# First attention of a twelve-stage decoder: the weighing moves between the second and the third turning, and ScalarE's second copy moves behind three exponentials

## The chip, the cores and the metric

The kernel runs on one core of a Trainium2 chip. The metric is the device time of one launch in microseconds (us); less is better. The times shown are the median, the lowest and the highest of three runs. Engines: TensorE (PE in the profile, and PEld for its weight loads), VectorE (DVE), ScalarE (ACT), GpSimd (POOL), and SyncE (SP), which issues the loads.

## The reference

A decoder of four layers, each with self-attention, cross-attention and a feed-forward part, over x of 4 batches, 512 positions and 128 features. Only the first self-attention is touched by the change. Per batch and with x normalised:

```
qkv = x @ W_attn + b_attn                    # 16 heads of 8 features
att = (q @ k.T) / sqrt(8) / temperature
att = att + slope[h] * (pos_k - pos_q), and -inf where pos_k > pos_q
w = softmax(att, axis=-1)
x = x + (w @ v) @ W_proj + b_proj
```

## The kernel before

The stages run one after the other; the first attention is the first of them, `l0_attention`. Its inner work is cut into 64 quads. Quad k belongs to batch b = k // 16, to query tile tt = (k % 16) // 4 of 128 queries, and to group g = k % 4. It holds four heads r = 0 to 3 (`R`), and works on the (tt + 1) * 128 keys that the causal mask leaves, so that a quad of tt = 3 is four times as wide as one of tt = 0. In this text quad number n of a batch is k % 16.

Each quad passes through these steps:

- `score` on TensorE (L415): four matmuls, one for each head, into banks 0 to 3. It waits until all four masks of the quad before are done.
- `mask` on VectorE (L240), one for each head: adds the position bias, takes the row minimum and writes `sc`.
- `exponent` on ScalarE (L353), one for each head: writes `pr`.
- `turn` on TensorE (L426), one for each head: (tt + 1) transposes of 128x128 into one of two banks. Heads 0 and 2 share bank 4 and heads 1 and 3 share bank 5, so a turning waits for the copy of the turning before it in its bank.
- `copy`, which frees the bank: heads 0 and 2 on ScalarE (L345), heads 1 and 3 on VectorE (L250). It writes `prT`, of which there are two sets (`RING` = 2).
- `weigh` on TensorE (L443 and L447): probabilities times v, and times ones for the sums. It waits for all four copies of its quad.
- After every fourth quad VectorE divides (reciprocal L267, product L271) once `weigh` of that quad's fourth group is done. It does so at the head of its iteration k, three quads later, ahead of `mask(k, 0)`; that is where k % 4 = 2, from k = 6 on.

The steps are ordered by one loop written out on each engine, each with its own program of iterations k, and semaphores between them. In iteration k TensorE scores quad k, turns quad k - 1 and weighs quad k - 2. VectorE masks quad k and copies quad k - 1. ScalarE copies quad k - 1 and takes the exponentials of quad k.

In iterations with n = 4 to 12 of the first three batches one piece of the next batch's projection is done as well (`project`, L394, and for the ninth, v, L397). For the first eight pieces ScalarE then takes the result out of its bank (`take`, L327 and L330, which waits for the projection) and rounds it (`round_high`, L337), and GpSimd finishes it. VectorE takes the ninth out. In iteration n = 3 of each later batch, and once after the last quad, TensorE also does the output projection of the batch before (L471), and VectorE adds it to X (L290).

Of the kernel before, what the change touches and what calls it, by code (L numbers as in the profile page):

```python
# [159 lines left out]
def l0_attention(nc, T, A):  # L160
    H, HD = 16, 8
    G, R = 4, 4
    QUADS = B * TPB * G
# [6 lines left out]
    with Stage(nc, T, "l0a") as st:  # L170
# [32 lines left out]
        def place(k):  # L203

            b, n = divmod(k, PER)
            return b, n // G, n % G

        def piece_at(k):

            b, n = divmod(k, PER)  # L210
            return [(b + 1, n - FIRST)] if b + 1 < B and 0 <= n - FIRST < PIECES else []

        def home(b, n):

            return T.bank[n % 8] if b == 0 else pbank

        with nc.Block() as block:
# [96 lines left out]
            @block.scalar  # L314
            def _(act):
                def take(b, n):

                    g, kind = divmod(n, 2)
                    act.wait_ge(projected, PIECES * b + n + 1)
                    done = 2 * G * b + n - 4  # L320
                    if done >= 0:
                        if kind:
                            act.wait_ge(split_k, done // 2 + 1)
                        else:
                            act.wait_ge(split_q, done // 2 + 1)
                    if kind:
                        nc.scalar.activation(raw[:, n % 4, :], home(b, n)[:, :], ACT.Identity, bias=cols[:, G + g:G + g + 1])\  # L327
                            .then_inc(taken, 1)
                    else:
                        nc.scalar.activation(raw[:, n % 4, :], home(b, n)[:, :], ACT.Identity, bias=qbias[:, g:g + 1],  # L330
                                             scale=qscales[:, g:g + 1]).then_inc(taken, 1)

                def round_high(b, n):

                    g, kind = divmod(n, 2)
                    act.wait_ge(taken, 2 * G * b + n + 1)
                    nc.scalar.activation(qk[:, b % 2, kind, g, :], raw[:, n % 4, :], ACT.Copy).then_inc(high, 1)  # L337

                def copy(j, r):

                    W = (place(j)[1] + 1) * P
                    act.wait_ge(turned, R * j + r + 1)
                    if j >= RING:
                        act.wait_ge(pv_done, j - RING + 1)
                    nc.scalar.activation(prT[:, j % RING, r, 0:W], tbank[0][:, 0:W], ACT.Copy).then_inc(copied_a, 1)  # L345

                def exponent(k, r):

                    W = (place(k)[1] + 1) * P
                    act.wait_ge(masked, R * k + r + 1)  # L350
                    if k >= RING:
                        act.wait_ge(turned, R * (k - RING) + r + 1)
                    nc.scalar.activation(pr[:, k % RING, r, 0:W], sc[:, k % RING, r, 0:W], ACT.Exp,  # L353
                                         bias=nmx[:, k % RING, r:r + 1], scale=-1.0).then_inc(expd, 1)
                act.wait_ge(loaded, 16 * len(loads))
                act.wait_ge(prepared, 1)
                for n in range(2 * G):
                    take(0, n)
                    if n:
                        round_high(0, n - 1)  # L360
                round_high(0, 2 * G - 1)
                for k in range(QUADS + 1):
                    if k >= 1:
                        copy(k - 1, 0)
                    if k < QUADS:
                        exponent(k, 0)
                    if k >= 1:
                        copy(k - 1, 2)
                    if k < QUADS:
                        for r in range(1, R):  # L370
                            exponent(k, r)
                    for b, n in piece_at(k):
                        if n < 2 * G:
                            take(b, n)
                            round_high(b, n)

            @block.tensor
            def _(pe):
# [22 lines left out]
                def score(k):  # L401

                    b, tt, g = place(k)
                    W = (tt + 1) * P
                    if tt == 0:
                        pe.wait_ge(split_q, G * b + g + 1)
                        pe.wait_ge(split_k, G * b + g + 1)
                    if k >= 1:
                        pe.wait_ge(masked, R * k)
                    else:  # L410
                        pe.wait_ge(taken, 2 * G)
                        pe.wait_ge(v_ready, 1)
                    for r in range(R):
                        m = slice(32 * r, 32 * r + 32)
                        out = nc.tensor.matmul(sbank[r][:, 0:W], qk[m, b % 2, 0, g, tt * P:(tt + 1) * P], qk[m, b % 2, 1, g, 0:W],  # L415
                                               start=True, stop=True)
                    out.then_inc(scored, 1)

                def turn(j, r):

                    pe.wait_ge(expd, R * j + r + 1)
                    before = 2 * j + r // 2
                    if before:
                        pe.wait_ge(copied_v if r % 2 else copied_a, before)
                    for t in range(place(j)[1] + 1):
                        out = nc.tensor.transpose(tbank[r % 2][:, t * P:(t + 1) * P], pr[:, j % RING, r, t * P:(t + 1) * P],  # L426
                                                  T.ident[:, :])
                    out.then_inc(turned, 1)

                def weigh(j):  # L430

                    b, tt, g = place(j)
                    pe.wait_ge(copied_a, 2 * j + 2)
                    pe.wait_ge(copied_v, 2 * j + 2)
                    if tt == 0 and g == 0:
                        pe.wait_ge(v_ready, b + 1)
                    if g == 0 and j // G >= 1:
                        pe.wait_ge(yT_ready, j // G)
                    for t in range(tt + 1):
                        first, end = g == 0 and t == 0, g == G - 1 and t == tt  # L440
                        for r in range(R):
                            m, c = slice(32 * r, 32 * r + 32), r * G * STRIDE + g * R * HD
                            nc.tensor.matmul(obank[m, 0:P], v[:, b % 2, t, c:c + R * HD],  # L443
                                             prT[:, j % RING, r, t * P:(t + 1) * P], start=first, stop=False)
                        for r in range(R):
                            m = slice(32 * r, 32 * r + 32)
                            out = nc.tensor.matmul(obank[m, P:2 * P], ones[:, g * R * HD:(g + 1) * R * HD],  # L447
                                                   prT[:, j % RING, r, t * P:(t + 1) * P], start=False, stop=end)
                    out.then_inc(pv_done, 1)
# [4 lines left out]
                for k in range(QUADS + 4):  # L454
                    if k < QUADS:
                        score(k)
                    for r in range(R if 1 <= k <= QUADS else 0):
                        turn(k - 1, r)
                    for b, n in piece_at(k):
                        project(b, n)  # L460
                    if 2 <= k < QUADS + 2:
                        weigh(k - 2)
                    if k >= PER and k % PER == 3:
                        b = k // PER - 1
                        pe.wait_ge(yT_ready, TPB * b + TPB)
                        if b + 1 < B:
                            pe.wait_ge(v_ready, b + 2)
                        else:
                            pe.wait_ge(added, b)
                        for t in range(TPB):  # L470
                            out = nc.tensor.matmul(pbank[:, t * D:(t + 1) * D], yT[:, b % 2, t * P:(t + 1) * P], wproj[:, :],  # L471
                                                   start=True, stop=True)
                        out.then_inc(out_ready, 1)
# [2128 lines left out]
```

## Time and profile before

| | us |
|---|---|
| median of 3 runs | 2660.39 (2655.98 to 2660.68) |
| the profiled execution's own time | 2660.01 |
| its span, first to last instruction | 2658.2 |
| first score of the stage to first score of its last quad | 32.5 to 288.6 |
| last weighing of the stage ends, reciprocal starts | 299.8 |

The span is made of stages with different limits; the first attention is a tenth of it. Its quads have no loads from memory in them, so that they are read from the timeline of the three engines. What sets a quad's length is the distance from one `score` to the next.

### The profile page before, as it was taken

The page shows a single profiled execution, that of the slowest core. Times are in us where ns is not written, and L with a number is a line of the kernel's source. Part 1 is how long each engine was busy: PE and PEld are TensorE (multiplying, and loading weights), DVE is VectorE, ACT ScalarE, POOL GpSimd, SP SyncE. Part 2 cuts the span into 40 slices and gives each one's busy share as a digit, 9 for nine tenths or more (in the row PEclk, how much of TensorE's full clock was granted, in tenths as well). Part 3 has the DMA queues.
Part 4 walks back from the last instruction along what each step waited for, and adds up shares of the span by engine and source line. Part 5 has one row for each costly group of instructions (what it writes and reads, how often), then busy time and mean ns, then how long its engine had stood idle before and what let it go on. Part 6 is the DMA issues. An engine that isn't in the chain of part 4 may idle for free. (4 is left out here: it accounts for less than half of the span.)

```text
span 2658.2 us, 43969 instructions
## 1 busy us (share of the span) xinstructions
PE 2227.7 (84%) x13502; PEld 1582.2 (60%) x13502; DVE 1791.3 (67%) x3827; ACT 1241.8 (47%) x2557; POOL 1196.4 (45%) x1377
## 2 busy tenths in 40 slices
PE   6888759663999975749999999989999867699698
PEld 3666547453788853636656556655666445499555
DVE  4667658556688856666776676767677555477598
ACT  6777535222566642225445344534444432244365
POOL 5331028001699920127666565756575100022298
PEclk8999869775999998769999999999999977699799
DMA  1000024000666600013344343334333400000184
GB/s 45 2 2 2 7 57 100 7 6 19 140 153 153 150 4 18 1 63 80 80 84 92 77 98 75 96 65 96 77 84 79 87 6 0 32 1 1 25 176 101
DMA packets 63008, 162.17 MB, mean 61 GB/s; under 512 B 7563, under 2 KB 18571, under 8 KB 55000
## 3 DMA queue, kind: packets, MB, share of 16 engines
q1 hardware_dynamic: 62792, 159.50, 26.8%
q8 instruction: 110, 1.80, 0.3%
q14 instruction: 106, 0.87, 0.1%
HBM read 156.46 MB, written 3.01 MB: 60 GB/s over the span
## 5 line engine op out<-in xcount | busy, mean ns | idle before, releaser
L1984 PE MATMUL bank<-l2h_og,l2h_wo 128*128 128x512 f32 x512 | 264.2, 600 | 12.0 <-DVE LNT L2228 11.3
L2086 ACT ACTIVATE l2h_pr<-twin,l2h_nmx 128x512 f32<-128x512 f32 x256 | 176.0, 688 | 173.6 <-PE bank L1973 122.3
L2078 ACT ACTIVATE l2h_prT<-bank 128x512 f32<-128x512 f32 x256 | 151.7, 592 | 213.1 <-PE bank L1973 213.1
L1075 POOL TENSOR_TENSOR l1m_hid_lo<-l1m_hid,l1m_hid_hi 128x512 fp32r<-128x512 f32 x136 | 217.2, 1617 | 62.1 <-ACT l1m_hid_hi L1054 61.4
L2231 DVE TENSOR_REDUCE l2h_nmx<-twin 128x2 f32<-128x1024 f32 x128 | 156.2, 1220 | 104.5 <-PE twin L1963 103.8
L2204 DVE TENSOR_TENSOR l2h_vg<-bank,l2h_gv 128x512 f32<-128x512 f32 x256 | 175.4, 685 | 54.6 <-POOL l2h_vs L2299 32.0
L2299 POOL TENSOR_TENSOR l2h_vs<-l2h_vg 128x256 f32<-128x256 f32 x256 | 190.8, 745 | 27.9 <-DVE l2h_vg L2204 27.7
L2294 POOL TENSOR_TENSOR l2h_plain<-l2h_plain,l2h_rotated 128x512 f32<-128x512 f32 x64 | 82.0, 1281 | 213.9 <-DVE l2h_rotated L2197 213.9
L2216 DVE TENSOR_TENSOR l2h_og<-bank,l2h_gt 128x512 f32<-128x512 f32 x256 | 173.2, 680 | 5.3 <-PE bank L1984 2.7
L1973 PE MATMUL bank<-ident,l2h_pr 128*128 128x128 f32 x1024 | 163.4, 282 | 2.5 <-issue 2.5
L1973 PEld LDWEIGHTS bank<-ident,l2h_pr 128*128 128x128 f32 x1024 | 119.0, 143 | 71.4 <-issue 54.8
L1948 PE MATMUL bank<-l2h_w_hi,l2h_x_hi 128*128 128x512 f32 x256 | 151.5, 592 | 4.8 <-DVE l2h_vg L2204 3.7
L1114 DVE TENSOR_TENSOR l1m_hid<-l1m_prod,l1m_c 128x512 f32<-128x512 f32 x128 | 132.5, 1035 | 5.6
L2302 POOL TENSOR_TENSOR l2h_vs<-l2h_vs 128x128 f32<-128x128 f32 x256 | 124.2, 485 | 20.1
L353 ACT ACTIVATE l0a_pr<-l0a_sc,l0a_nmx 128x128 f32<-128x128 f32 (+3 forms) x256 | 128.9, 553 | 8.0 <-DVE l0a_nmx L240 7.7
L426 PE MATMUL bank<-ident,l0a_pr 128*128 128x128 f32 x640 | 105.3, 288 | 29.7 <-ACT l0a_prT L345 23.6
L118 PE MATMUL bank<-ident,LNX 128*128 128x128 f32 x112 | 27.6, 425 | 119.3 <-ACT LNX L127 98.7
L1048 ACT ACTIVATE l1m_gate<-bank 128x512 f32<-128x512 f32 x136 | 81.3, 598 | 93.7 <-PE bank L1009 93.7
L1997 PE MATMUL bank<-l2h_prT,l2h_v 128*64 128x256 f32 x1024 | 124.6, 385 | 0.0
L1984 PEld LDWEIGHTS bank<-l2h_og,l2h_wo 128*128 128x128 f32 x512 | 95.4, 190 | 43.2 <-issue 18.1
L1075 POOL TENSOR_TENSOR l3m_hid_lo<-l3m_hid,l3m_hid_hi 128x512 fp32r<-128x512 f32 x68 | 107.8, 1615 | 27.8 <-ACT l3m_hid_hi L1054 27.6
L2307 POOL TENSOR_TENSOR l2h_v<-l2h_vs 128x64 f32<-128x64 f32 x256 | 83.0, 324 | 71.4 <-PE bank L1997 53.7
(636 smaller groups left out, 6199.1 us busy)
## 6 DMA issues: line engine op xcount, KB each, us to landing
l2h_gt<-l2m_gate_rows SPq DMA_DIRECT2D x128, 512.0 KB, 7.1
l1m_c<-l1m_weights SPq DMA_DIRECT2D x64, 512.0 KB, 6.3
l3m_c<-l3m_weights SPq DMA_DIRECT2D x32, 512.0 KB, 6.6
l0m_c<-l0m_weights SPq DMA_DIRECT2D x16, 512.0 KB, 6.8
l1m_w<-in_l1m_pairs SPq DMA_DIRECT2D x32, 192.0 KB, 6.2
l2h_fresh<-in_l2m_wqkv SPq DMA_DIRECT2D x8, 768.0 KB, 4.9
l2h_wo<-in_l2m_wo SPq DMA_DIRECT2D x8, 512.0 KB, 4.8
l0m_w<-in_l0m_pairs SPq DMA_DIRECT2D x8, 192.0 KB, 5.0
```

The costliest lines, as they stand in the source:

```text
L353: nc.scalar.activation(pr[:, k % RING, r, 0:W], sc[:, k % RING, r, 0:W], ACT.Exp, bias=nmx[:, k % RING, r:r + 1], scale=-1.0).then_inc(exp ...
L1075: nc.gpsimd.tensor_tensor(hid_lo[:, at, :], hid[:, (n + PRE) % 4, :], hid_hi[:, at, :], ALU.subtract)\
L1114: nc.vector.tensor_tensor(h, prod[:, n % 2, :], cslot[s][:, blk * S:(blk + 1) * S], ALU.mult)\
L1948: out = nc.tensor.matmul(pj[at % 2][:, :], x[:, b * S + t * P:b * S + (t + 1) * P], w[:, QK + h * S:QK + (h + 1) * S], start=(p == 0), sto ...
L1973: out = nc.tensor.transpose(tbank[:, c * P:(c + 1) * P], pr[:, h, c * P:(c + 1) * P], T.ident[:, :])
L1984: nc.tensor.matmul(ybank[:, :], wo[s][:, e, :], og[:, e % 4, :], start=(e == 0), stop=(e == E - 1))\
L2078: nc.scalar.activation(prT[:, j // 2 % 2, h, :, j % 2 * P:(j % 2 + 1) * P], tbank[:, :].rearrange("p (c q) -> p c q", c=TPB), ACT.Copy).th ...
L2086: nc.scalar.activation(pr[:, h, :], sbank[:, h, :], ACT.Exp, bias=nmx[:, k % 2, h:h + 1], accum_out=rs[:, g % 2, t, h:h + 1]).then_inc(exp ...
L2204: nc.vector.tensor_tensor(vg[:, u % 2, :, :], pj[at % 2][:, :].rearrange("p (e d) -> p e d", e=E), spread(gv_h[s][:, b * TPB + t, h, :], H ...
L2216: nc.vector.tensor_tensor(og[:, e % 4, :], obank[g % 2][:, :], gt[:, e // 4, e % 4, :], ALU.mult)\
L2231: nc.vector.tensor_reduce(nmx[:, k % 2, :], sbank[:, :, :], axis=AX, op=ALU.max, negate=True)\
L2299: nc.gpsimd.tensor_tensor(vs[:, u % 2, :, :], vg[:, u % 2, 0:4, :], vg[:, u % 2, 4:8, :], ALU.add)\
```

## The change

On TensorE `weigh` of the quad two steps back now stands between the second and the third turning, ahead of the projection piece. On ScalarE the copy of head 2 goes behind the exponentials of heads 0, 1 and 2. Nothing is added or left out, and the waits inside each step are the same.

```diff
@@ ScalarE
                     if k >= 1:
                         copy(k - 1, 0)
                     if k < QUADS:
-                        exponent(k, 0)
+                        for r in range(3):
+                            exponent(k, r)
                     if k >= 1:
                         copy(k - 1, 2)
                     if k < QUADS:
-                        for r in range(1, R):
-                            exponent(k, r)
+                        exponent(k, 3)
                     for b, n in piece_at(k):
                         if n < 2 * G:
                             take(b, n)
@@ TensorE
                     if k < QUADS:
                         score(k)
-                    for r in range(R if 1 <= k <= QUADS else 0):
+                    for r in range(2 if 1 <= k <= QUADS else 0):
+                        turn(k - 1, r)
+                    if 2 <= k < QUADS + 2:
+                        weigh(k - 2)
+                    for r in range(2, R if 1 <= k <= QUADS else 0):
                         turn(k - 1, r)
                     for b, n in piece_at(k):
                         project(b, n)
-                    if 2 <= k < QUADS + 2:
-                        weigh(k - 2)
```

## Rows read from the trace of the kernel before

**Rows 1.** The page: busy us, share and instructions of each engine

```profile
PE 2227.7 (84%) x13502; PEld 1582.2 (60%) x13502; DVE 1791.3 (67%) x3827; ACT 1241.8 (47%) x2557; POOL 1196.4 (45%) x1377
```

**Rows 2.** Waits, 34 to 300 us: total us, times, longest

```profile
ACT l0a_prT L345 <- PE bank L426: 48.3, 75, 2.8
...
PE bank L426 <- ACT l0a_prT L345: 23.6, 64, 0.7
...
DVE l0a_rinv L267 <- PE bank L447: 12.5, 10, 3.0
```

**Rows 3.** Timeline of quad 27 (tt = 2, with a piece): start, us, engine

```profile
140.66 0.44 PE L415 MATMUL bank<-l0a_qk 32*128 32x384 f32 x2
...
141.03 0.87 PE L426 MATMUL bank<-ident,l0a_pr 128*128 128x128 f32 x6
141.34 0.56 DVE L240 CUSTOM_DVE_ANT_0 l0a_sc<-l0a_rel,bank 128x384 f32<-128x384 f32 x1 [1.70 <-PE twin L415]
141.62 0.49 ACT L345 ACTIVATE l0a_prT<-bank 128x384 f32<-128x384 f32 x1 [0.41 <-PE bank L426]
...
142.25 0.92 PE L426 MATMUL bank<-ident,l0a_pr 128*128 128x128 f32 x6 [0.34 <-ACT l0a_prT L345]
...
143.96 0.43 PE L443 MATMUL bank<-l0a_prT,l0a_v 128*32 128x128 f32 x8
...
144.72 0.67 ACT L327 ACTIVATE l0a_raw<-bank,l0a_cols 128x512 f32<-128x512 f32 x1
...
145.41 0.50 PE L415 MATMUL bank<-l0a_qk 32*128 32x512 f32 x2
```

**Rows 4.** Windows of one core: engines' busy us, granted clock (third number from the end)

```profile
108.50:112.00 3.50, 3.34 (x26) 2.67 (x26) 1.08 (x8) 1.55 (x6) 0.00 (x0) 0.52 0.00 0
...
112.10:127.10 15.00, 12.72 (x149) 7.13 (x148) 10.06 (x43) 13.24 (x31) 8.52 (x6) 1.00 0.01 2
127.10:145.40 18.30, 16.49 (x232) 10.56 (x228) 12.75 (x42) 16.80 (x33) 11.38 (x8) 1.00 0.01 2
248.40:260.00 11.60, 9.36 (x141) 6.08 (x140) 10.06 (x43) 8.84 (x23) 0.00 (x0) 1.00 0.01 2
```

**Rows 5.** Timeline: the scores that open quads 20 and 24

```profile
112.11 0.38 PE L415 MATMUL bank<-l0a_qk 32*128 32x256 f32 x2
...
127.13 0.44 PE L415 MATMUL bank<-l0a_qk 32*128 32x384 f32 x2
```

**Rows 6.** Timeline of quads 30 (with a division) and 31, tt = 3

```profile
154.67 0.50 PE L415 MATMUL bank<-l0a_qk 32*128 32x512 f32 x2
...
154.86 0.95 DVE L267 RECIPROCAL l0a_rinv<-bank 128x128 f32<-128x128 f32 x1
...
156.05 0.68 DVE L240 CUSTOM_DVE_ANT_0 l0a_sc<-l0a_rel,bank 128x512 f32<-128x512 f32 x1
...
156.65 0.69 DVE L250 COPY l0a_prT<-bank 128x512 f32<-128x512 f32 x1
...
159.92 0.50 PE L415 MATMUL bank<-l0a_qk 32*128 32x512 f32 x2
...
160.36 1.09 PE L426 MATMUL bank<-ident,l0a_pr 128*128 128x128 f32 x8
...
161.79 1.16 PE L426 MATMUL bank<-ident,l0a_pr 128*128 128x128 f32 x8 [0.34 <-ACT l0a_prT L345]
...
162.88 0.43 PE L443 MATMUL bank<-l0a_prT,l0a_v 128*32 128x128 f32 x8
...
164.77 0.33 PE L415 MATMUL bank<-l0a_qk 32*128 32x128 f32 x2
```

**Rows 7.** Timeline of the stage's last turnings (iteration 64), with TensorE's weight loads

```profile
293.46 0.86 PEld L426 LDWEIGHTS bank<-ident,l0a_pr 128*128 128x128 f32 x8 [0.20 <-issue]
...
294.87 0.95 PEld L426 LDWEIGHTS bank<-ident,l0a_pr 128*128 128x128 f32 x8 [0.55 <-issue]
...
295.99 0.16 PEld L443 LDWEIGHTS bank<-l0a_prT,l0a_v 128*32 128x32 f32 x8 [0.17 <-issue]
...
296.10 0.69 DVE L250 COPY l0a_prT<-bank 128x512 f32<-128x512 f32 x1 [0.81 <-PE bank L426]
```

## The prediction, made before the changed kernel ran

> **What bounds the kernel now.** I read the page first. In a span of 2658.2 us it shows no engine that is always busy: TensorE leads with 84% [rows 1]. Shares over twelve stages say nothing of this change, so I went to the first attention alone. The list of waits for that stretch names the wait that the change is aimed at: TensorE stood before a turning, because ScalarE had not yet copied the one before it out of the bank, 64 times, once in each quad, 23.6 us in all [rows 2]. The timeline shows the place. In quad 27 the first two turnings start at 141.03, ScalarE's copy of head 0 at 141.62, and the third turning at 142.25, 0.34 us after TensorE was free for it [rows 3]. The quad runs from 140.66 to 145.41, 4.75 us, and this is TensorE's only wait for another engine in it. In quad 31 it is the same 0.34 us [rows 6]. So TensorE sets the pace, with a hole of 0.34 us in each quad.
>
> The windows say how far off the other engines are. Over quads 20 to 23 (112.10 to 127.10) ScalarE is busy 13.24 us of 15.00, more than TensorE's 12.72. Over quads 24 to 27 both are near: 16.80 and 16.49 of 18.30. In 248.40 to 260.00, which has no projection pieces, VectorE leads with 10.06 of 11.60 [rows 4]. A gain on TensorE will therefore soon meet ScalarE or VectorE.
>
> A second hole is the division. In quad 30 VectorE starts the reciprocal 0.19 us after the score (154.86 against 154.67), since it waited for the weighing at the end of the iteration before, and masks only at 156.05, 1.38 us after the score, where quad 27 has 0.68 [rows 3]. The quad takes 5.25 us against 4.85 for quad 31 [rows 6]: 0.4 us, in 15 quads. That wait of the reciprocal is also in the list, 12.5 us [rows 2].
>
> **The change, part by part.** No instruction is added or removed, so the price lies in waits alone.
>
> *The weighing between turnings two and three.* The third turning needs a copy that comes 1.22 us after the first turning in quad 27 (141.03 to 142.25) and 1.43 us in quad 31. A weighing of this width takes 1.45 us (143.96 to 145.41) [rows 3], of tt = 3 1.89 us (162.88 to 164.77) [rows 6]. It covers the copy, and the 0.34 us go. That is the upper bound: 64 x 0.34 = 21.8 us.
>
> *One more change of matmul shape.* Before, a quad without a piece goes score (32 rows), turning (128x128), weighing (128x32). Now it has a return from weighing to turning and a step from turning to score. Weight loads stand idle 0.20 us from a weighing to a turning, 0.17 us from a turning to a weighing, and 0.55 us across the wait for the copy [rows 7]. One hole of 0.55 is replaced by one more gap of about 0.2, which gives the same 0.35; the matmul rows' 0.34 is thus net of it. The step from a turning to a score is not in the trace. I take 0.2, the nearest rows; the low bound is nothing, the high one that it is as dear as the present hole, 0.55, 0.35 more than taken.
> The Trainium skill speaks against the change here: "Changing tiling mode (not just tile) drains the TensorE" (TensorEngine Tiling (Array Packing), Key Properties). The trace agrees, with gaps near 0.2 us at such changes; by the page one more drain per quad takes part of the gain, and by the rows it is already counted.
>
> *The division with a piece in the quad.* The weighing that it waits for ends before the last turnings, so VectorE can divide while TensorE does the piece (from 0.8 us after the third turning to 143.96, near 0.95 us [rows 3]). The stall, between the 0.4 of quad 30 and the 0.7 by which its first mask is late, goes in 6 such quads.
>
> *Quads 20 to 23 (tt = 1, with pieces).* They take 15.02 us (112.11 to 127.13) [rows 5]. Without 4 x 0.34 and a division stall of 0.65 (near the 0.7, since quads are short here) TensorE would need 13.0. ScalarE's 13.24 us of busy time are the floor, and its take now waits for a projection at the end of the iteration, so I put 13.5: **gain 1.5**.
>
> *Quads 24 to 27 (tt = 2).* 18.28 us (127.13 to 145.41) [rows 3, 5]. Less 1.36 and a stall of 0.5 is 16.4, and 0.2 for ScalarE, which arrives late from the quads before: 16.6, **gain 1.7**. Here the moved take starts at about the next score rather than at 144.72; the copy of head 0 then comes late by some 0.5 us, inside the cover of the weighing.
>
> *Quads 28 to 31 (tt = 3).* Together 19.36 us (145.41 to 164.77) [rows 3, 6]. Quad 28 has v's piece and gains the full 0.34. In quad 29 VectorE's masks become the limit (I put 4.15 against 4.41): 0.26. In quad 30 the division gets worse cover: VectorE's copy of head 3 can start 1.23 us after the third turning (294.87 to 296.10), a weighing or now the next score 1.12 us after it [rows 7]. So copy (0.6) and division (156.05 - 154.86 = 1.19) end 1.9 us after the score, where the first mask is now at 1.38 [rows 6]. From there to the next score VectorE needs five steps of 0.6 (156.05 to 156.65) and the handover, 3.1: 5.03 against 5.25, 0.22. In quad 31 the copy of head 2, now behind three exponentials, is late for the next first turning, which takes back most: 0.06. **Gain 0.9.**
>
> *Quads 16 to 19 (tt = 0).* The turnings of the wide quad 15 pass without a wait (0.24), but the first two turnings of iteration 17 now follow the wide copies after only a narrow score, where a wide weighing stood between: -0.16. The other two come out even, +0.07. **Gain 0.15.**
>
> *The last batch has no pieces.* Between copy of head 2 and the next first turning only turnings and a score are left (1.12 + 0.43 in quad 31), and the round trip from a turning by its copy to the next in its bank is 1.43 [rows 6, 7]; at tt = 1 and 2 the copy stands behind `exponent` of head 2, so that 0.15 to 0.3 of the 0.34 come back as a wait of turning 0. VectorE is near its limit there as well [rows 4]. I put 0.1 for its eight middle quads, 0.5 from division quads and 0.7 for the rest: **gain 1.3**.
>
> *The end.* After the last turnings nothing covers their copies: weighing 63 must wait 1.23 + 0.69 + 0.15 = 2.07 us from turning 2, where 1.12 us of turning [rows 7] and a weighing of 1.9 lay in between. 0.95 lost, 0.34 saved: **loss 0.6**.
>
> Sum: batches 1 and 2 give 0.15 + 1.5 + 1.7 + 0.9 = 4.25 each; batch 0, whose first quads have no wide quad before them and run at half clock, 3.9; batch 3 1.3; end -0.6. 8.5 + 3.9 + 1.3 - 0.6 = **13.1 us**. The profiled execution took 2660.0 and would take 2646.9; its own time lies 0.4 under the median, so the median becomes 2647.3. GpSimd needs 8.52 us for the pieces of quads 20 to 23 and 11.38 for the next four [rows 4], under the new lengths.
>
> **Rivals.** *The waits only change names (same).* Turning 0 waits for copy 2 everywhere, as I expect only without pieces, and ScalarE is full in quads 20 to 27. For it: ScalarE waits 48.3 us for turnings [rows 2], which ties both engines in one loop. Against it: with a piece TensorE has 0.95 us more between turning 2 and the next turning 0. It gives a gain of 1 to 5: 2657.
>
> *The step from turning to score is dear (slower).* At the high bound, 0.35 more in the 37 quads without a piece and after a piece too, 63 x 0.35 = 22 us against a gain of 13: 2669. It decides from 13.1 / 63 = 0.21 more per quad. Against it: all three changes of shape in the trace cost 0.17 to 0.24.
>
> *The clock.* The granted clock is 0.52 in 108.50 to 112.00, half speed (1.2 GHz of 2.4), after the sparse quad 18 [rows 4], and such a stretch stands in quads 19, 35 and 51. Each costs up to 3.4 / 2 = 1.7 us. If denser quads end them, 5 us more are gained: 2642. I leave quads 17 and 18 as they are, so it is unlikely.
> The Trainium skill says that "activity releases the throttle" (TensorE: Matmul & The Clock Gate, What's actually happening); the trace agrees, and that rule would favour this rival.
>
> *No second limit.* TensorE alone counts: 21.8 plus 15 x 0.5 of division: 29 us, 2631. The windows [rows 4] speak against it.
>
> **How the numbers follow.** Chances: forecast (gain 8 to 17) 0.56, clock 0.13, no second limit 0.04, names only 0.20, slower 0.07. 0.2% is 5.3 us, about what the measurement can tell from no change. Faster: 0.56 + 0.13 + 0.04 and a part of the names-only case, 0.75; same 0.18; slower 0.07. The range is the forecast's own on both sides, stretched to the clock case and to the lower end of names-only: 2640 to 2656.
>
> **What would show it.** The wait of L426 for L345 falls from 23.6 to under 8 us in total. Quads 24 to 27 take near 16.6 us, quads 20 to 23 near 13.5, with the reciprocal of quads 22 and 26 before their score. Turning 0 shows new waits for the copy of head 2 in the last batch, and the last weighing comes 0.6 us later against its turnings. The prediction is wrong if weight loads idle over 0.3 us ahead of a score, if ScalarE's take holds up the third turning, or if the half-clock stretches multiply.

## The result, and the profile after

The changed kernel takes 2637.56 us (median of 4 runs, 2637.26 to 2639.68); the kernel before, beside it, 2659.22 us (4 runs). The ratio is 0.9922, with a 95% interval of 0.9905 to 0.9939. The change saves 21.7 us. The prediction had the sign and the mechanism, but forecast 13.1 us, and 2637.6 lies below its range. All medians in this text are of fast executions; one slow one, 6505 us in `scalar_only`, is left out.

The page of the changed kernel shows the same work in a shorter span (columns as in [rows 1]):

```profile
span 2635.7 us, 43969 instructions
...
PE 2219.5 (84%) x13502; PEld 1581.4 (60%) x13502; DVE 1793.2 (68%) x3827; ACT 1241.6 (47%) x2557; POOL 1198.7 (45%) x1377
```

The list of waits over the stage, here 34 to 280 us, answers to [rows 2]:

```profile
ACT l0a_prT L345 <- PE bank L426: 20.6, 49, 2.3
ACT l0a_pr L353 <- DVE l0a_nmx L240: 17.8, 42, 0.8
...
PE bank L426 <- ACT l0a_prT L345: 7.0, 25, 0.8
...
PE bank L443 <- DVE l0a_yT L271: 2.9, 4, 0.9
```

TensorE's wait for ScalarE's copies fell from 23.6 to 7.0 us and from 64 times to 25. ScalarE's own waits moved: 48.3 us for turnings became 20.6, and its wait for VectorE's masks rose from 7.7 to 17.8. The last line is new: `weigh` now waits for the division.

The timeline of quad 27 of the changed kernel, beside [rows 3]:

```profile
128.01 0.44 PE L415 MATMUL bank<-l0a_qk 32*128 32x384 f32 x2
...
128.38 0.64 PEld L426 LDWEIGHTS bank<-ident,l0a_pr 128*128 128x128 f32 x6 [0.18 <-ACT l0a_pr L353]
...
129.19 0.43 PE L443 MATMUL bank<-l0a_prT,l0a_v 128*32 128x128 f32 x8
...
129.59 0.47 ACT L345 ACTIVATE l0a_prT<-bank 128x384 f32<-128x384 f32 x1
...
130.63 0.64 PEld L426 LDWEIGHTS bank<-ident,l0a_pr 128*128 128x128 f32 x6 [0.20 <-ACT l0a_pr L353]
130.64 0.87 PE L426 MATMUL bank<-ident,l0a_pr 128*128 128x128 f32 x6
...
131.24 0.30 PEld L394 LDWEIGHTS bank<-LNT,l0a_w 128*128 128x128 f32 x2
...
132.30 0.18 PEld L415 LDWEIGHTS bank<-l0a_qk 32*128 32x128 f32 x2 [0.76 <-issue]
132.30 0.50 PE L415 MATMUL bank<-l0a_qk 32*128 32x512 f32 x2
...
132.41 0.69 ACT L327 ACTIVATE l0a_raw<-bank,l0a_cols 128x512 f32<-128x512 f32 x1
```

The first turning starts at 128.38 and the weighing at 129.19, 0.81 us later. In [rows 3] the third turning stood 1.22 us after the first. The copy of head 0 starts late, at 129.59, as foreseen (1.21 us after its turning, 0.59 before), and the third turning at 130.64 does not wait for it. The quad takes 4.29 us instead of 4.75.

Adding up the distances from score to score gives the table. It compares the two profiled executions; the last column is what the prediction had for the same quads.

| quads | before | after | saved | predicted |
|---|---|---|---|---|
| 0 to 15 | 64.3 | 58.9 | 5.4 | 3.9 |
| 16 to 19 | 15.3 | 13.3 | 1.95 | 0.15 |
| 20 to 23 | 15.0 | 13.2 | 1.8 | 1.5 |
| 24 to 27 | 18.3 | 16.2 | 2.1 | 1.7 |
| 28 to 31 | 19.4 | 18.0 | 1.3 | 0.9 |
| 32 to 47 | 68.2 | 60.8 | 7.4 | 4.25 |
| 48 to 62 | 55.7 | 53.5 | 2.1 | 1.3 |
| score of quad 63 to the last reciprocal | 11.15 | 11.99 | -0.84 | -0.6 |

From the first score to that of quad 63 the stage went from 256.1 to 233.9 us, 22.2 us less; from the first score to the start of the last reciprocal it went from 267.2 to 245.9 us, 21.3 us less. It also began 1.8 us earlier, which is not the change's doing (below).

What lies behind that reciprocal is the same code in every kernel of this study, yet it took between 2353 and 2359 us in the twelve traces (2358.5 in the kernel before, 2359.1 in the changed kernel, 2353.3 in `split_weigh`). A difference of a few us between two medians can therefore come from outside the changed stage, and below each such difference is set beside the stage's own length.

Windows of the changed kernel, columns as in [rows 4]. The first row covers quads 18 and 19, the second quads 20 to 23, the last two quads 50 and 51:

```profile
98.00:101.40 3.40, 2.49 (x38) 1.56 (x41) 2.80 (x16) 2.24 (x8) 0.00 (x0) 1.00 0.02 5
...
102.90:116.10 13.20, 12.37 (x149) 7.19 (x148) 10.23 (x43) 12.17 (x30) 7.32 (x6) 1.00 0.01 2
...
219.00:222.40 3.40, 2.21 (x30) 1.42 (x30) 2.93 (x14) 2.36 (x8) 0.00 (x0) 1.00 0.01 2
222.50:225.90 3.40, 3.40 (x28) 2.69 (x26) 1.27 (x10) 1.83 (x6) 0.00 (x0) 0.52 0.02 5
```

The half-clock stretch stands in quad 51 as before, but is gone from quads 19 and 35: these fell from 4.50 and 4.62 us to 2.73 and 2.66.

### The profile page after: what moved, and what is told of

The parts are those of the page before. It is cut to its first block and busy times, and to the rows that moved or that the text cites. A ratio compares the mean times of both kernels' runs of the same rounds, so it can differ in the third digit from the quotient of the medians.

```text
span 2635.7 us, 43969 instructions
## 1 busy us (share of the span) xinstructions
PE 2219.5 (84%) x13502; PEld 1581.4 (60%) x13502; DVE 1793.2 (68%) x3827; ACT 1241.6 (47%) x2557; POOL 1198.7 (45%) x1377
## 3 DMA queue, kind: packets, MB, share of 16 engines
HBM read 156.46 MB, written 3.01 MB: 61 GB/s over the span
## 5 line engine op out<-in xcount | busy, mean ns | idle before, releaser
L353 ACT ACTIVATE l0a_pr<-l0a_sc,l0a_nmx 128x128 f32<-128x128 f32 (+3 forms) x256 | 133.7, 556 | 18.5 <-DVE l0a_nmx L240 17.8
L1112 DVE TENSOR_TENSOR l1m_prod<-bank,l1m_gate 128x512 f32<-128x512 f32 x128 | 88.2, 689 | 37.5 <-ACT l1m_gate L1050 37.2
```

## The experiments

### One part alone

Each half of the change was run by itself. `tensor_only` has TensorE's half:

```diff
-                    for r in range(R if 1 <= k <= QUADS else 0):
+                    for r in range(2 if 1 <= k <= QUADS else 0):
+                        turn(k - 1, r)
+                    if 2 <= k < QUADS + 2:
+                        weigh(k - 2)
+                    for r in range(2, R if 1 <= k <= QUADS else 0):
                         turn(k - 1, r)
...
-                    if 2 <= k < QUADS + 2:
-                        weigh(k - 2)
```

> Only TensorE's part of the change: the weighing between turnings two and three, ScalarE's order as before. Theory A (the weighing takes the hole in every quad, and ScalarE's copy of head 2 must stand late because it now waits for a turning that comes after the weighing): ScalarE stands before that copy with three exponentials behind it, so the quads of tt = 1 and 2 with a piece grow by 0.3 to 0.8 us against the changed kernel and the kernel takes 2643 to 2652. Rival B (the order on ScalarE does not matter, TensorE is the only pace-maker): 2637 to 2639, as the changed kernel.

Measured: 2637.62 us (4 runs), ratio to the kernel before 0.9925 (0.9908 to 0.9941), the same as the whole change. I had held theory A, and it fell as to the time. Its mechanism was there, though: quads 20 to 23 take 13.70 us against 13.21 with both halves, and quads 24 to 27 16.82 against 16.18. What I had left out is that the quads without a piece are faster than in the changed kernel (quad 31 4.40 against 4.63, quad 55 2.52 against 2.79). This takes back a part, and chance, in the traces, the rest: the profiled execution of `tensor_only` had no half-clock stretch in quad 51 (2.85 us, against 4.24 in the changed kernel). Its stage is 246.2 us long against 245.9; without that 1.4 us it would be 1.7 us the longer.

`scalar_only` has ScalarE's half:

```diff
                     if k < QUADS:
-                        exponent(k, 0)
+                        for r in range(3):
+                            exponent(k, r)
...
-                        for r in range(1, R):
-                            exponent(k, r)
+                        exponent(k, 3)
```

> Only ScalarE's part: the copy of head 2 behind three exponentials, TensorE's order as before. Theory A: each quad keeps its wait for the copy of head 0 (about 23 us in total), and the copy of head 2 is covered by the weighing that still follows the turnings: no change, 2657 to 2661. Rival B: the exponentials that come earlier free the turnings of the next quad and give part of the gain by themselves, 2650 or less.

Measured: 2659.09 us (9 runs, 2655.03 to 2664.34), ratio 1.0004 (0.9992 to 1.0016). Theory A. By itself the order on ScalarE gives nothing. In its trace quads 9, 25 and 41 even grew from 4.32 to 4.54 us. Its stage was 7.4 us longer than before, and it had more of half clock: a stretch of 20.5 us in the first quads instead of 13.6, and one of 17 us from quad 51 on instead of 3.4.

### How many exponentials ahead of the copy

`two_exps` is the changed kernel with the copy of head 2 one place earlier:

```diff
                     if k < QUADS:
-                        for r in range(3):
+                        for r in range(2):
                             exponent(k, r)
                     if k >= 1:
                         copy(k - 1, 2)
                     if k < QUADS:
-                        exponent(k, 3)
+                        for r in range(2, R):
+                            exponent(k, r)
```

> The changed kernel with ScalarE's copy of head 2 behind two exponentials instead of three. Theory A: in quads without a piece the wait of the first turning for this copy (behind the third exponential) falls, 0.1 to 0.2 us in about 30 quads, and in quads with a piece little changes: 2633 to 2637. Rival B: the copy then stands at the head of ScalarE's queue waiting for turning 2 with two exponentials behind it, so ScalarE falls behind in the quads with pieces: 2640 or more.

Measured: 2632.68 us (4 runs, 2632.26 to 2633.35), ratio 0.9904 (0.9888 to 0.9921). It is 4.9 us below the changed kernel, slightly more than theory A had, and its slowest execution is faster than the fastest of either kernel. Of this the stage explains a part: first score to last reciprocal is 244.5 us against 245.9, 1.4 us less, and 2.8 without the half-clock stretch that this trace had in quad 35 (4.03 us against 2.67). The stage does not explain the rest. It has the better half of each neighbour: quads 20 to 23 take 13.19 us and 24 to 27 16.17, as with three exponentials, and quads 31 and 55 take 4.39 and 2.52, as with one. The weight loads of the turning after the score of quad 31 show the reason. In the changed kernel:

```profile
144.63 0.86 PEld L426 LDWEIGHTS bank<-ident,l0a_pr 128*128 128x128 f32 x8 [0.20 <-issue]
145.68 0.18 PEld L415 LDWEIGHTS bank<-l0a_qk 32*128 32x128 f32 x2 [0.19 <-DVE l0a_nmx L240]
...
146.38 0.75 PEld L426 LDWEIGHTS bank<-ident,l0a_pr 128*128 128x128 f32 x7 [0.51 <-issue]
```

and at the same score with two exponentials:

```profile
144.63 0.18 PEld L416 LDWEIGHTS bank<-l0a_qk 32*128 32x128 f32 x2 [0.19 <-DVE l0a_nmx L240]
...
145.07 0.88 PEld L427 LDWEIGHTS bank<-ident,l0a_pr 128*128 128x128 f32 x8 [0.25 <-issue]
```

With three, the first turning's loads stand idle for 0.51 us after the score: the copy of head 2 came behind the third exponential. With two they stand 0.25 us, which is the usual gap there. The first block also prices a change of matmul shape: 0.20 us from weighing to turning, and 0.19 from turning to score, the step that the trace of before did not have (a mask was waited for there as well; where none was, at 100.15, it is 0.22).

### The price of a change of shape

`split_weigh` is the changed kernel with the weighing cut in two:

```diff
-                def weigh(j):
+                def weigh(j, half):
...
+                    cut = (tt + 1) // 2 if tt else 1
+                    if half and not tt:
+                        return
...
-                    for t in range(tt + 1):
+                    for t in range(cut, tt + 1) if half else range(cut):
...
                     if 2 <= k < QUADS + 2:
-                        weigh(k - 2)
+                        weigh(k - 2, 0)
                     for r in range(2, R if 1 <= k <= QUADS else 0):
                         turn(k - 1, r)
+                    if 2 <= k < QUADS + 2:
+                        weigh(k - 2, 1)
                     for b, n in piece_at(k):
                         project(b, n)
```

> The changed kernel with the weighing of a quad of tt = 1, 2 or 3 cut in two: its first key tiles between turnings two and three, the others right behind turning four. The work is the same; TensorE changes the shape of its matmuls twice more in 48 quads (turning to weighing, and weighing to projection or score). Theory A (a change of shape costs the gap of 0.17 to 0.24 us that the weight loads show, and no more): quads of tt = 2 and 3 grow by 0.15 to 0.4 us, and the time by 6 to 13 us to 2643 to 2651. Rival B (a change of shape costs more than the gap shows, 0.4 us or more each): 20 us and more, 2657 or above. Rival C (the gaps would be there without a change of shape too): 2637 to 2640.

Measured: 2643.16 us (4 runs, 2641.03 to 2647.96), 5.6 us above the changed kernel, at the lower end of theory A. The stage itself grew by more, from 245.9 to 255.5 us, in the middle of it. The weight loads of its quad 27:

```profile
134.30 0.18 PEld L415 LDWEIGHTS bank<-l0a_qk 32*128 32x128 f32 x2 [0.76 <-issue]
...
134.68 0.64 PEld L426 LDWEIGHTS bank<-ident,l0a_pr 128*128 128x128 f32 x6 [0.19 <-issue]
135.48 0.16 PEld L446 LDWEIGHTS bank<-l0a_prT,l0a_v 128*32 128x32 f32 x8 [0.17 <-issue]
...
136.34 0.64 PEld L426 LDWEIGHTS bank<-ident,l0a_pr 128*128 128x128 f32 x6 [0.49 <-issue]
137.15 0.16 PEld L446 LDWEIGHTS bank<-l0a_prT,l0a_v 128*32 128x32 f32 x8 [0.17 <-issue]
...
138.16 0.30 PEld L394 LDWEIGHTS bank<-LNT,l0a_w 128*128 128x128 f32 x2 [0.20 <-issue]
139.21 0.18 PEld L415 LDWEIGHTS bank<-l0a_qk 32*128 32x128 f32 x2 [0.76 <-issue]
```

The two added changes cost 0.17 and 0.20 us, and the quad grew by 0.63 (4.92 against 4.29). The other 0.26 is no price of the shape: the gap ahead of turning three is 0.49 us instead of 0.20, since one key tile's weighing is too short to cover the copy. In quads 28 to 31, three of them without a piece, the sum grew by 0.56 only, 0.47 of it in quad 28. So such a change of shape is 0.2 us, and rival B, on which "slower" rested, is out. So is rival C: in quad 27 of the changed kernel the projection's loads follow the turning's, of the same shape, without a gap (131.24), and here, behind a weighing, 0.20 us late (138.16). The Trainium skill's statement that a change of tiling mode drains TensorE (TensorEngine Tiling (Array Packing), Key Properties) agrees with these gaps of 0.17 to 0.20 us.

One gap is larger. Behind the projection, whose matmuls have 512 columns, the next loads stand idle for 0.76 us (134.30 and 139.21 above, 132.30 in the changed kernel). That is more than the 0.3 us ahead of a score that the prediction named as a sign of being wrong, but it is no new cost: in the kernel before it stood ahead of the weighing, a fourth change of shape beside the three that the prediction counted. Quad 27 there:

```profile
142.90 0.30 PEld L394 LDWEIGHTS bank<-LNT,l0a_w 128*128 128x128 f32 x2
143.96 0.16 PEld L443 LDWEIGHTS bank<-l0a_prT,l0a_v 128*32 128x32 f32 x8 [0.76 <-ACT l0a_prT L345]
```

### The clock

Three runs ask whether the half-clock stretches belong to the sparse quads at a batch's start. `before_filled` adds matmuls, whose result is not used, to TensorE's waits there, in the kernel before:

```diff
+                def fill(k, r):
...
+                    n = S if k % PER == 2 and r == 2 else S // 2
+                    pe.wait_ge(v_ready, k // PER + 1)
+                    nc.tensor.matmul(pbank[:, 0:n], w[:, 0:P], T.LNT[:, 0:n], start=True, stop=True)
...
                         turn(k - 1, r)
+                        if k > PER and 1 <= k % PER <= 3 and k < QUADS and 1 <= r <= 2:
+                            fill(k, r)
```

> The kernel before with added matmuls whose result is not used (a projection weight against the first 256 or 512 columns of x, into the bank of the output projection, which is overwritten later) in TensorE's waits of quads 17, 18, 19, 33, 34, 35, 49, 50 and 51. Theory A (the half-clock stretch in quads 19, 35 and 51 follows from TensorE's sparse quads before it): the granted clock stays 1.00 there, those quads fall from 4.5 to 4.6 us to about 3.1, and the time falls by 3 to 5 us to 2654 to 2657. Rival B (the half-clock stretches come by chance, and the changed kernel missed two by where they fell): they stand there as before or elsewhere, and the time is the same or up to 2 us more, 2659 to 2662.

Measured: 2652.65 us (10 runs, 2647.94 to 2659.85), ratio 0.9983 (0.9972 to 0.9994). Theory A as to the clock. After 52 us no stretch is left in the stage; quads 19, 35 and 51 take 3.49 us each instead of 4.5 to 4.6 (3.1 had been expected), though quads 17, 33 and 49 pay 0.38 for the fill. These nine quads save 2.0 us net; the median lies 5.4 us lower, below theory A's 2654, and the nine quads do not explain all of it.

> The kernel before once more, for its trace. Theory A (the half-clock stretch belongs to the sparse quads at the start of a batch): granted clock at half in quads 19, 35 and 51 as in the first trace. Rival B (chance): other quads, or fewer of them. The start of the stage (first score at 32.5 us) may move by up to 2 us with the clock, which is at half for part of the first projections in one trace and not in another.

> The changed kernel once more, for its trace. Theory A (denser quads hold the clock up): at most one half-clock stretch in quads 16 to 62, and where one falls it is in quad 19, 35 or 51. Rival B: three stretches as in the kernel before, so that the 3.3 us of quads 19 and 35 were chance.

Each was executed once, for its trace: 2655.91 us the kernel before, 2637.10 the changed one. In the second trace of the kernel before, quad 19 kept its clock and took 3.13 us; quads 35 and 51 had the stretch (4.47 and 4.55). Its windows of quads 34 and 35:

```profile
172.90:176.30 3.40, 2.07 (x27) 1.11 (x25) 2.66 (x16) 2.17 (x8) 0.00 (x0) 0.96 0.00 0
176.30:179.70 3.40, 3.40 (x30) 2.60 (x30) 0.90 (x7) 1.37 (x5) 0.00 (x0) 0.54 0.00 0
```

The second trace of the changed kernel repeated the first: one stretch, in quad 51. Over all traces with TensorE's old order and no fill (two of the kernel before, and `scalar_only`) the stretch stood in 8 of the 9 places; with the new order (two of the changed kernel, `tensor_only`, `two_exps`, `split_weigh`, and `best_plain` below) in 7 of 18. It is rarer, and not excluded. Theory A holds in this form only.

The first score stood at 32.5 us in both traces of the kernel before and at 30.5 to 30.7 in both of the changed one, but also at 32.73 in `tensor_only` and at 30.35 in `scalar_only`. The code up to there is the same in all. The difference lies in the first projections: their first four or five matmul records take 1.06 us each in the traces that start late and 0.59 in the others, like all later ones. In the kernel before the clock records of the trace begin, at full clock, only at 23.1 us, just behind the records of 1.06 us, in the changed kernel at 17.6; so half clock is the likely cause. It follows no order of the loop.

### Better versions

`best_filled` goes on from `two_exps`:

```diff
+                def fill(k):
...
+                    pe.wait_ge(v_ready, k // PER + 1)
+                    for n in (S, S // 2):
+                        nc.tensor.matmul(pbank[:, 0:n], w[:, 0:P], T.LNT[:, 0:n], start=True, stop=True)
...
+                    late = k == QUADS
                     for r in range(2 if 1 <= k <= QUADS else 0):
                         turn(k - 1, r)
-                    if 2 <= k < QUADS + 2:
+                    if k > PER and k % PER == 2 and k < QUADS:
+                        fill(k)
+                    if 2 <= k < QUADS + 2 and not late:
                         weigh(k - 2)
...
                         project(b, n)
+                    if late:
+                        weigh(k - 2)
```

> The kernel with the copy of head 2 behind two exponentials, with two things more: in quads 18, 34 and 50 two matmuls whose result is not used stand in the wait of the weighing for the division (0.9 us long, the matmuls take about 0.65), and the last but one weighing stands behind the last turnings, as before the change. Theory A (the half-clock stretches in quads 35 and 51 come from TensorE's sparse quads just before): none is left in quads 16 to 62, quads 19, 35 and 51 take 2.5 us each, and the end of the stage is 0.8 us shorter: 2629 to 2632. Rival B (they fall by chance): one or two stretches remain and the gain is the 0.8 us of the end alone, 2631.5 to 2633.

Measured: 2631.28 us, but over 2624.62 to 2636.14 in 4 runs, so it was run again beside the same kernel without the added matmuls:

> The kernel with the copy of head 2 behind two exponentials, and the last but one weighing behind the last turnings as before the change; no added matmuls. Theory A (half-clock stretches in quads 35 and 51 remain in most executions): 2631.5 to 2633. Rival B (they come by chance and their mean cost is small): the same as the kernel with the added matmuls within 1 us.

> The same with the two added matmuls whose result is not used in quads 18, 34 and 50, timed again beside it. Theory A: 1.5 to 3 us less than the kernel without them, 2629 to 2631. Rival B: no difference beyond 1 us, because the clock of other stages varies by more than this from one execution to the next.

Measured: 2636.00 us (6 runs, 2629.79 to 2639.24), ratio 0.9920 (0.9907 to 0.9933), without them; 2631.11 us (4 runs, 2629.53 to 2632.54), ratio 0.9902 (0.9887 to 0.9916), with them. Without them theory A's 2631.5 to 2633 is missed: this is `two_exps` with a shorter end, and its stage is 244.1 us against 244.5, yet its median is 3.3 us higher. So the 2632.68 of `two_exps` is not a firm figure either. The windows of quads 34 and 35 and of 50 and 51, without the added matmuls:

```profile
158.20:161.60 3.40, 2.49 (x36) 1.69 (x40) 2.94 (x16) 2.56 (x10) 0.00 (x0) 0.96 0.00 0
161.60:165.00 3.40, 3.40 (x29) 2.67 (x20) 1.32 (x9) 1.47 (x5) 0.00 (x0) 0.54 0.00 0
219.60:223.00 3.40, 2.40 (x30) 1.50 (x30) 2.92 (x14) 2.56 (x9) 0.00 (x0) 0.96 0.01 2
223.00:226.40 3.40, 3.40 (x31) 2.75 (x30) 1.38 (x10) 1.85 (x7) 0.00 (x0) 0.54 0.02 5
```

and of quads 34 and 35 with them:

```profile
158.20:161.60 3.40, 3.26 (x30) 1.90 (x30) 2.69 (x14) 2.24 (x8) 0.00 (x0) 1.00 0.00 0
161.60:165.00 3.40, 3.40 (x51) 2.51 (x51) 2.78 (x15) 2.38 (x9) 0.00 (x0) 1.00 0.00 0
```

The added matmuls in quad 18, with them:

```profile
97.64 0.43 PE L427 MATMUL bank<-ident,l0a_pr 128*128 128x128 f32 x2
97.91 1.46 PE L455 MATMUL bank<-LNT,l0a_w 128*128 128x512 f32 x4
99.29 0.43 PE L444 MATMUL bank<-l0a_prT,l0a_v 128*32 128x128 f32 x8
```

They take 1.4 us, not the 0.65 that was expected, and so do not fit into the wait of 0.9: quads 18, 34 and 50 grow from 2.76 to 3.01 us. With them TensorE is busy 3.26 of 3.40 us ahead of quad 35 and the clock stays at 1.00; without, 2.49, and it falls to half. From the first score to that of quad 63 the traces read 230.9 and 232.9 us. Of the 4.9 us between the medians, 1.9 are thus seen in the stage; the rest lies in other stages, which are the same code, and the intervals overlap. The filled version is the fastest of the study, by an amount that stays open between none and 5 us.

The weighing put back behind the last turnings brought the end from 11.75 us in `two_exps` to 11.27 (the kernel before has 11.15): 0.5 us, where 0.8 had been expected. The changed kernel's 11.99 fell to 11.75 by the place of the copy alone.

## Why the prediction was wrong in its size

**What held.** The hole in each quad was what the change removes, and TensorE's half removes it (`tensor_only`, while `scalar_only` gives nothing). The wait fell to 7.0 us, under the 8 that were named. The shape's price was right (`split_weigh`). The division with a piece moved ahead of the score: the reciprocal of quad 22 starts at 108.85 with the score at 109.26, and quads 22 and 26 save 0.98 us each. The expected comeback of the wait behind the third exponential is there (0.51 us of idle weight loads at quad 31), and `two_exps` removes it. The end lost 0.84 where 0.6 was predicted.

**The term that was too small.** The step that failed is the sentence that one hole of 0.55 us is replaced by a gap of about 0.2 and that "the matmul rows' 0.34 is thus net of it". The matmul row's wait is less than the hole. In quad 27 the distance from first turning to the next step on TensorE went from 1.22 to 0.81 us: 0.41; with 0.05 between the third turning and the projection the quad saves 0.46, and quads 28, 39 and 43 0.47, 0.53 and 0.46. The weight loads said so before the run: 0.55 - 0.17 = 0.38 [rows 7], while I took the other neighbour, 0.2. That is 0.07 to 0.13 us too little in a quad that TensorE sets. Of the nine quads 20 to 28 seven saved 0.41 or more; quad 21 lost 0.15 and quad 25 saved 0.14 only. Over the 20 such quads in the three batches with pieces this is an estimated 1.5 to 2.5 of the 8.6 us.

**Limits that were set too early.** ScalarE was to hold quads 20 to 23 at 13.5 us and they took 13.2. In the window of the changed kernel (102.90 to 116.10, above) ScalarE is busy 12.17 us with 30 instructions, against 13.24 with 31 in [rows 4]. About half of the difference is one more `take` at the window's edge, cut off after 0.52 us; the same 16 exponentials took 0.28 us less in sum, and the rest is open. So the busy time of a window was no floor. In quad 30 VectorE allowed 4.87 us, not 5.03, and in quad 31 4.63, not 4.79. Together with the first term this makes 5.6 us over the stage: 19.3 us saved without the clock, where the same sum had 13.7 (1.5, 1.6, 1.7 and 0.8 us more than predicted in batches 0 to 3). No run separates what each limit gave of it.

**The clock.** It was a rival with a chance of 0.13 and a price of 5 us for three stretches, on the ground that quads 17 and 18 stay as they are. They did (6.11 us before, 6.19 after), yet two of three stretches went. Quad 19 took 3.13 us at full clock in the second trace of the kernel before, so the clock's share of its 1.77 us is 1.4; with quad 35 alike, 2.9 us. The range took this case and the forecast as alternatives; they came together, and with too small a forecast. The rows show a busier TensorE ahead of the places where the clock held (2.49 of 3.40 us, against 2.21 in the same kernel where it fell, and 2.07 in the kernel before), and added matmuls make it hold. But in `best_plain` it fell behind 2.49 as well, so these rows do not tell beforehand where it falls; that stays open.

**A missed wait.** The weighing of the first of four groups waits for the division of the quad before. Placed earlier, it meets that division on TensorE's path in quad 18 of the changed kernel:

```profile
97.84 0.56 PE L426 MATMUL bank<-ident,l0a_pr 128*128 128x128 f32 x2
99.15 0.42 PE L443 MATMUL bank<-l0a_prT,l0a_v 128*32 128x128 f32 x8 [0.75 <-DVE l0a_yT L271]
...
100.15 0.21 PEld L415 LDWEIGHTS bank<-l0a_qk 32*128 32x128 f32 x2 [0.22 <-issue]
```

The last line is the change from turning to score named above. The quad takes 2.76 us with this wait and took 2.78 before, so it costs nothing net; it is the hole into which the added matmuls were put.

The sum of the profiled executions: 22.2 us in the stage to quad 63, of them 2.9 of clock, less 0.84 at the end, plus 1.8 from the slower first projections of the kernel before, which is chance, less 0.6 in all other stages: 22.5 us of span.

## What to carry to other kernels

When a wait is replaced by work, size the hole from the idle time of the weight loads, and not from the wait that is written at the matmul; here the loads said 0.38 us, the matmul row 0.34, and quad 27 gave 0.46. Move independent work into a round trip between two engines, and then look for the next round trip that lost its cover: one place on ScalarE's queue was worth 1.4 us in the stage, 2.8 without a half-clock stretch, and of the three places tried the middle one was the best. Differences of this size are read from the stage itself: the same code outside it varied by 6 us. A hole in a sparse stretch can cost twice, once as a wait and once as the clock behind it.

## What the runs showed of the hardware that I had not expected

The same program, at the same quad, kept full clock in one execution (quad 19, 3.13 us) and fell to half in another (4.50 us), and two added matmuls of 1.4 us in all, at a wait of 0.9 us, kept it up in all three places of both traces that had them. Weight loads of 128 x 128 after 32-column tiles start 0.20 us behind them, those of the weighing 0.17 us behind the turnings, and those of the score 0.19 to 0.22 us, so that these three shapes pay about 0.2 us per change in any order; only behind the 512 columns of the projection is it 0.76.
